# Two chained convolution layers on one core: the final 1x1 of the first layer issued in halves of three units, with two of its squares one group later

## What is computed

```python
# layer 0
g = _gn(x)                                        # group norm, 32 groups of 16 channels
f = relu(einsum('oc,nchw->nohw', Wc, g) + bc)     # 1x1, 512 -> 128
# a dynamic 3x3 kernel per image, from the mean and the cell maxima of g
dynW = relu(einsum('oj,ncjkl->nockl', Wck, gs) + bck)
y = conv3x3(f, dynW) + b_ad                       # 128 -> 128, kernel of its own per image
x1 = x + einsum('oc,nchw->nohw', Wf, y) + bf      # the final 1x1, 128 -> 512
# layer 1
out = x1 + grouped_conv3x3(_gn(x1), kernels)      # 32 groups of 16 -> 16 channels
```

## Time and profile before

| | before |
|---|---|
| median of 3 runs | 3552.5 us |
| the profiled execution's own time | 3549.79 us |
| its span in the trace | 3548.0 us |
| granted TensorE clock, mean | 0.994 |
| TensorE busy | 3453.4 us (97%) |
| VectorE busy | 2551.1 us (72%) |
| ScalarE busy | 2108.9 us (59%) |
| GpSimd busy | 966.6 us (27%) |
| DMA queue q1, share of 16 engines | 69.8% |

### The profile page before, as it was taken

One profiled execution on the slowest core, in us unless ns is written; L12 is line 12 of the kernel. 1 busy time (PEld: TensorE's weight loads), 2 busy tenths in 40 slices (PEclk: granted clock), 3 DMA queues, 4 the chain that ended last, 5 costly groups with the idle time before them and its releaser, 6 DMA issues.

```text
span 3548.0 us, 60228 instructions
## 1 busy us (share of the span) xinstructions
PE 3453.4 (97%) x18688; PEld 2804.6 (79%) x18688; DVE 2551.1 (72%) x5365; ACT 2108.9 (59%) x3559; POOL 966.6 (27%) x1039
## 2 busy tenths in 40 slices
PE   5799999999999999999999999999999999999996
PEld 4688888788888888888888888888887888888785
DVE  7677777776777777777677777767777777777742
ACT  3366555675565665655665556755556655556654
POOL 2133222233222232222332222332222332222323
PEclk9899999999999999999999999999999999999998
DMA  5567767777767677777677777677676777676666
GB/s 124 149 194 192 194 184 186 205 201 182 200 184 198 195 189 185 203 190 198 190 191 194 194 183 206 198 189 199 178 192 202 197 183 204 182 201 194 172 147 167
DMA packets 317577, 666.88 MB, mean 188 GB/s; under 512 B 58863, under 2 KB 288242, under 8 KB 288645
## 3 DMA queue, kind: packets, MB, share of 16 engines
q1 hardware_dynamic: 317317, 663.34, 69.8%
HBM read 355.00 MB, written 308.28 MB: 187 GB/s over the span
## 4 chain that ended last, share of the span: by engine, by line
PE 97%; DVE 1%; DMA 1%; issue 0%; POOL 0%; ACT 0%; SPq 0%; POOLq 0%; ACTq 0%
PE pb L853 16%; PE pb L854 16%; PE pb L855 16%; PE pac L853 8%; PE pac L854 8%; PE pac L855 8%; PE pd L853 7%; PE pd L855 7%; PE pd L854 7%; PE pac L927 2%; PE pac L862 1%; PE ps L920 1%; DVE bst L604 0%; DVE mx L612 0%; PE ps L921 0%
## 5 line engine op out<-in xcount | busy, mean ns | idle before, releaser
L407 POOL TENSOR_TENSOR hl<-un,hl 128x384 f16<-128x384 f32 x1024 | 938.9, 917 | 2501.7 <-ACT hl L432 2498.7
L432 ACT ACTIVATE hl<-un 128x384 f16<-128x384 f32 x1024 | 538.9, 526 | 399.5 <-PE pb L855 331.3
L428 ACT ACTIVATE un<-big,b_t,s_t 128x384 f32<-128x384 f32 x1024 | 709.8, 693 | 15.7 <-DMA big<-x_rows 15.7
L764 DVE SCALAR_TENSOR_TENSOR x1b<-pac,bfc,big 128x384 f32<-128x384 f32 x768 | 424.0, 614 | 193.9 <-PE pac L855 193.5
L853 PE MATMUL pb<-fh,dynh 128*128 128x480 f32 (+3 forms) x1440 | 543.8, 378 | 0.0
L854 PE MATMUL pb<-fl,dynh 128*128 128x480 f32 (+3 forms) x1440 | 541.1, 376 | 0.0
L855 PE MATMUL pb<-fh,dynl 128*128 128x480 f32 (+3 forms) x1440 | 540.8, 376 | 0.0
L853 PE MATMUL pd<-hl,k_h 128*96 128x376 f16 (+1 forms) x1536 | 508.7, 331 | 18.4 <-POOL hl L407 18.4
L853 PE MATMUL pb<-hl,k_h 128*96 128x376 f16 (+1 forms) x1536 | 506.9, 330 | 0.0
L854 PE MATMUL pd<-hl,k_h 128*96 128x376 f16 (+1 forms) x1536 | 506.6, 330 | 0.0
L855 PE MATMUL pd<-hl,k_l 128*96 128x376 f16 (+1 forms) x1536 | 506.6, 330 | 0.0
(11 more groups left out here) (115 smaller groups left out, 5272.5 us busy)
## 6 DMA issues: line engine op xcount, KB each, us to landing
big<-x SPq DMA_DIRECT2D x128, 1152.0 KB, 10.0
x_rows<-x1b SPq DMA_DIRECT2D x128, 1152.0 KB, 5.6
big<-x_rows SPq DMA_DIRECT2D x128, 1152.0 KB, 12.6
out<-big SPq DMA_DIRECT2D x128, 1152.0 KB, 6.3
big<-x_rows SPq DMA_DIRECT2D x256, 192.0 KB, 13.1
x_rows<-mrow SPq DMA_DIRECT2D x64, 96.0 KB, 1.9
big<-kt SPq DMA_DIRECT2D x4, 288.0 KB, 10.7
big<-kt SPq DMA_DIRECT2D x2, 192.0 KB, 11.2
```

The source lines that it names most:

```text
L407: pool.tensor_tensor(hl[:, g % HL_RING, 1, :, 1:W + 1], un[:, g % U_RING], hl[:, g % HL_RING, 0, :, 1:W + 1], ALU.subtract).then_inc(hl_lo, 1)
L428: act.activation(un[:, g % U_RING], t_slot(g // GQ)[:, g % GQ], ACT.Identity, bias=b_t[:, g:g + 1], scale=s_t[:, g:g + 1]).then_inc(u_done, 1)
L432: act.activation(hl[:, g % HL_RING, 0, :, 1:W + 1], un[:, g % U_RING], ACT.Copy).then_inc(hl_hi, 1)
L764: vec.scalar_tensor_tensor(out=x1b[:, c % X1_SLOTS, k, :].rearrange("p (b w) -> p b w", w=W), in0=pac[:, u % C_BANKS, 0:BW].rearrange("p ( ...
```

## The change

The table `C_AT` now gives, for a round, the units themselves. Chunks 0, 1 and 2 come in two halves of three units in neighbouring rounds; chunk 3 stays whole in round 11. The squares of chunks 0 and 1 stand one group later; that of chunk 2 stays behind group 22.

```diff
-C_AT = {0: 0, 4: 1, 8: 2, 11: 3}
+C_AT = {0: range(0, 3), 1: range(3, 6), 4: range(6, 9), 5: range(9, 12), 8: range(12, 15), 9: range(15, 18), 11: range(18, 24)}
...
-SQUARE_AFTER = {6: 0, 14: 1, 22: 2}
+SQUARE_AFTER = {7: 0, 15: 1, 22: 2}
...
                 for r in range(PAIRS):
                     if r in C_AT:
-                        for u in range(C_AT[r] * OR_, (C_AT[r] + 1) * OR_):
+                        for u in C_AT[r]:
                             residual(n, odd, u)
...
                     if r in C_AT:
-                        for u in range(C_AT[r] * OR_, (C_AT[r] + 1) * OR_):
+                        for u in C_AT[r]:
                             c_unit(n, u)
```

## The result

The changed kernel takes 3615.15 us (median of 4 runs, 3612.72 to 3617.98) against 3552.25 us of the kernel before in the same measurement: a ratio of 1.018, with a 95% interval of 1.0167 to 1.0192. It is slower by 63 us, or 1.8%. The forecast was 3614 us, with a range of 3578 to 3652 us.

A forecast was written before the change was run, and what follows sets the result against it. TensorE, without idle time at 107.44 us per image, was taken as the bound. Two new waits, 31.5 + 29.5 = 61 us, on the median of 3552.5 us gave 3614 us, range 3578 to 3652 us.

The forecast's parts named there:

- The bound: TensorE in steady images: 107.44 us per image with no idle time, so a new order could take nothing away.
- First stall: Mean matmul (L908, round 7): TensorE waits about 1.05 us for VectorE's prep_means in images 1 to 30, 31.5 us.
- Second stall: Group 23 (pair 11): TensorE waits 0.95 us for GpSimd after the square of chunk 2, images 1 to 31, 29.5 us.
- Squares of chunks 0 and 1: Moving them one group later costs nothing; group 8 has 0.4 us to spare, group 16 holds only behind the mean-matmul wait.
- Writes: Later writes cost nothing: chunk 2 lands at 1842.6, wanted at 1842.8 plus the group 23 wait; chunk 1 has 2 us.
- Switching: TensorE changing between pairs and units costs nothing, since seven pairs and a chunk add up to 24.02 us.
- Image 0: First image, without pairs: VectorE's work is the same, cost taken as 0, between -3 and +3 us.
- Only one stall: Either the mean matmul or group 23 wait is hidden behind a mis-sized slack: about 3583 us; chance 11%.
- The load later than 7.7 us: Next image's chunk 0 load takes 10.0 us, making the mean-matmul wait 3.35 us: 3683 us; chance 7%.
- No cost: Enough matmuls queued ahead of the array hide the waits: 3552 us, less up to 5.7 us; chance 7%.
- The clock: TensorE keeps the full clock, its waits being about as short as image 0's 1.32 us wait, which left it at 1.00.
- the third rival: TensorE's clock falls at each of 61 waits, 5.7 us lost each time, 348 us: 3962 us; chance 3%.

The follow-up runs named there:

- both fixes: Changed kernel, all halves kept, with the square of chunk 2 behind group 23 and the mean matmul behind round 8: 3559.22 us, ratio 1.0021 to the kernel before.

## Why the prediction was right

**The bound.** "There is nothing that a new order could take away there" held: no kernel of this order got below the one before by what can be measured, and the loss is what waits per image cost. The period was forecast as 109.4 us and is 109.49.

**First stall, 1.05 us.** It is 1.02. Each link shows: the last residual later, the load's issue later, 7.8 us to land (7.7 taken), the wait of 2.2 us at L604, 12.49 us of unbroken work (12.67). That the sum is so close is in part luck: VectorE's work is 0.18 us shorter than forecast, and the longer step behind the wait, 0.10 us, wasn't in the sum. Its causes were tested alone: with chunk 1 halved and the load in time 0.46 us (0.4 forecast), with chunk 0 halved alone the full size, with the mean matmul a round later 4 of the 30 us were left. That the landing reaches TensorE one to one was tested by moving the load and nothing else: VectorE's wait and TensorE's are both 8.3 us longer there than in the changed kernel.

**Second stall, 0.95 us.** It is 0.98, in 31 images. The square alone brings it about (chunk 2 halved alone) and moving the square alone takes it away.

**Squares of chunks 0 and 1, nothing.** Right in the changed kernel, and the forecast's next thing to show, group 16 behind the first stall, came up once that stall was removed, at 5.5 us in 30 images.

**Writes, nothing.** Right in the changed kernel too. The forecast gave the write of chunk 2 a margin of 0.2 us and the second stall; with both stalls removed VectorE does wait for that write, in four of the steady images.

**Switching, nothing.** It held, but the reason given for it was none: the cost of a chunk had been worked out as what seven pairs leave of the 24.02 us, so the sum had to come out. The kernel with chunk 2 alone in halves shows it: the period grows from 107.44 to 108.45 us, by 1.01, of which 0.98 are the stall and 0.04 the longer step behind it.

**The rest of the sum.** 30 x 1.02 + 31 x 0.98 = 61.0 us, as forecast; the spans differ by 63.0. Image 0, taken as 0 with 3 us either way, is 1.1 us longer by the start of its kernel matmuls (135.73 against 134.59 us). The longer step behind the second wait, 0.04 us in 31 images, is 1.2 us more. Together that is 63.3 us, so the spans agree to 0.3 us. The forecast had neither of these two terms, and 3613.5 was rounded up: that the measured median came within 1.2 us of the forecast is closer than the working could promise. The longer row of `pac` L853 is in image 0: its wait for the write of chunk 2 grew, while the one before the means shrank.

**The rivals.** Only one stall: no. The load later than 7.7 us: no, it lands in 7.6 to 8.1 us in the steady images. No cost, by matmuls queued ahead of the array: no, every wait was paid in full. The clock: it held through all 61 waits, and the third rival falls for waits of a microsecond. Two windows of the changed kernel, one a whole period, the other from the first stall over the second (the clock is the number behind the busy times):

```profile
1740.00:1849.50 109.50, 107.79 (x586) 87.15 (x584) 79.47 (x168) 65.65 (x112) 29.39 (x32) 1.00 0.71 190
1858.70:1873.80 15.10, 14.23 (x86) 11.34 (x86) 9.36 (x26) 9.68 (x17) 5.75 (x7) 1.00 0.93 256
```

The lower mean, 0.993 for 0.994, comes from image 0: 0.55 and 0.70 in the windows 102:117 and 117:134 us, where the kernel before had 0.62 and 0.83. That is (0.07 x 15 + 0.13 x 17) x 2 = 6.5 us more at 1.2 GHz, in a stretch in which TensorE mostly waits, and the image is only 1.1 us longer. The Trainium skill, page "TensorE: Matmul & The Clock Gate", section "HAM oscillation — how this bites in real kernels", tells of waits for a DMA, some 3 to 5 us each, after which every next tile starts at the low clock. The kernel with the late load agrees, with 9 us of idleness in each image and the clock at the lower level for 10.3 us around it. The waits of the changed kernel are much shorter than those of the section, and their trace shows no fall. So the prediction stretched the section when it read a price for its own stalls out of it.

**Where the forecast was off** is in one place of an experiment, not in its size: with chunk 0 alone halved I had the microsecond at L908, and it was at the banks. I had followed VectorE's list to the means and not asked TensorE's nearer wait, for a bank at the fourth unit of chunk 1. In the changed kernel a pair stands between the halves of chunk 1, 3 us in which VectorE frees the banks, so the same omission did no harm there.

## What to carry to other kernels

- Where the busiest engine has no idle time between images, and the change leaves its own work as it is, a new order can only cost. Look for what that engine takes just in time, here within 0.17 and 0.78 us, and follow each moved instruction to its last user. Here the two prices came out of starts and lengths of the trace to 0.03 us, though single terms were off by up to 0.18.
- When work moves later, ask what hangs on its end besides its own reader. Here the end of three residuals released a DMA write and, in the same queue, the load of the next image, which had been 0.7 us ahead of its reader.
- A late engine is paid for once, at the first place where the bound engine needs it. Moving one wait away shows the next: after both fixes 7 of 63 us stayed, most of them at a wait that had been hidden. For the same reason the prices of two causes on one engine don't add up: half a microsecond and one, taken alone, made one together.

## What the runs showed of the hardware

- Idle gaps of about 1 us, twice per image of 109.5 us, left the granted clock at 1.00. One gap of 9 us per image brought it to the lower level (1.2 GHz) for about 10 us in each image, and cost some 2.5 us beyond the wait itself.
- The idle time that the profile gives before a matmul is short of the loss by the overlap of two records: 0.75 against 0.92 us at L908, 0.81 against 0.98 at group 23. And a matmul behind a wait is itself followed a little later, 0.24 against 0.14 us at L908, 0.21 against 0.17 at group 23.
- Two transfers of 1152 KB issued 0.6 us apart land after 5.6 and 7.8 us; the same load issued 0.5 us behind the store of the outputs took 9.8 us, with the store at 6.3.
